# Feed-forward layer of a two-layer decoder on one core: weights in two float32r halves instead of three bfloat16 pieces

## The chip, the core and the metric

The kernel runs on one of the eight cores of a Trainium2 chip. A core has TensorE (PE: matrix multiplications, with weight loads shown apart as PEld), VectorE (DVE), ScalarE (ACT), GpSimd (POOL) and SyncE (SP), which here issues the DMAs. Each engine works through its own list of instructions in order; engines wait for one another on semaphores. The metric is the device time of one execution in microseconds (us). Three runs of the kernel before took 3097.56, 3102.97 and 3102.03 us; the median is 3102.03 us.

## The reference

Eight sequences of 256 tokens with 512 features pass through two decoder layers. Each layer has three sub-layers, and after each of them comes x = layernorm(x + sublayer(x)): windowed self-attention, quantised cross-attention and a GELU feed-forward in the first, a state-space layer with a convolution of four taps, linear attention and a mixture of experts in the second. The change touches the feed-forward:

```python
X = x.reshape(-1, H).astype(jnp.float16)
D = jnp.dot(X.astype(jnp.float32), W0.T) + bias0              # 512 -> 2048
D = jax.nn.gelu(D, approximate=False).astype(jnp.float16)
E = jnp.dot(D.astype(jnp.float32), W1.T) + bias1              # 2048 -> 512
return E.astype(jnp.float16).reshape(B, L, H)
```

The activations are float16 (11 significant bits) and the weights float32 (24 significant bits). float32r, a type that the changed kernel uses, is a float32 whose last 12 bits are zero.

## The kernel before

Eight stages run one after the other: self-attention (names with sa_), projections of the cross-attention (xp_), its heads (xh_), its output (xo_), the feed-forward (gf_), the state space (ss_), linear attention (la_) and the experts (ex_). Each stage is a block of hand-ordered programs, one per engine, and one block begins when every engine has ended the one before. A stage may fetch and prepare for the next one (`ahead`), and leaves its last normalisation to the next one (`behind.late_vector`, `late_pool`, `late_sync`). Batches are the eight sequences.

Feed-forward weights. `W0` and `W1` come in eight chunks of 128x2048 float32 (`fetch_chunk`), and each is split into three bfloat16 pieces whose sum is the float32: `top` (ACT, copies the chunk to bfloat16), `remainder` (DVE, subtracts it), `middle` (ACT, rounds the rest), `lowest` (DVE, subtracts again). Chunks 0 to 5 are split during the cross-attention's output stage, one per batch; chunks 6 and 7 are finished at the start of the feed-forward block. In the output stage each batch passes through one serial loop: SP loads `x` of the next batch into the buffer that the batch before it left, POOL adds the bias to it (L1328), POOL takes the inverse root (L77) for the batch at hand, DVE scales (L1274), SP stores and loads again.

Feed-forward block, for each batch n:

- PE first layer (L1566): 16 feature tiles x 4 contraction tiles x 3 pieces = 192 matmuls, a 128x128 weight tile each with 256 tokens of `xT` moving.
- PE turns the input of batch n+1 (`turn_input`, 8 transposes, L114). It needs `x_loaded`.
- PE second layer (L1579): 16 contraction tiles x 2 token tiles x 3 pieces = 96 matmuls, 128 tokens of `hid` as the loaded operand and 512 columns of `w1` moving.
- ACT copies the turned input to float16 (L1591) and applies GELU to the first layer's result, two tiles at a time (L1598); it writes float16, and PE reads that directly. `hid` has two buffers.
- DVE adds the bias and the residual when the second layer is done (L1622, L1625) and normalises; POOL takes the inverse root (L77). Then SP stores the batch (L1533) and, behind that in its list, loads `x` of batch n+2 (L1529).

Near the end of the block SP also fetches what the state-space stage needs: `w_in` (2 MB), the convolution's weight `w_conv` (4 MB), `w_x`, `w_dt` and `w_out`.

## Time and profile before

| | |
|---|---|
| runs, median | 3102.03 us |
| profiled execution: span from first to last instruction | 3090.6 us |
| mean granted TensorE clock | 0.969 |
| busy: PE / PEld / DVE / ACT / POOL | 91% / 59% / 67% / 48% / 35% |
| feed-forward, first matmul of the first layer | 1389.41 us |
| feed-forward, DVE takes the last result | 1731.72 us |

The profile gives no time of its own for the profiled execution beside its span; the median of the runs is 11.4 us above the span, which is the time around the first and the last instruction. The feed-forward lasts from 1386 to 1732 us, a ninth of the span. "Busy" PE in the profile means that at least one matmul is in flight, so its pace is read from start times, not from busy shares.

### The profile page before, as it was taken

How to read it: one execution, taken by the hardware profiler on the slowest of the kernel's cores; microseconds unless marked ns; L12 is line 12 of the kernel's file. 1: busy time of each engine (PE TensorE's matmuls, PEld its weight loads, DVE VectorE, ACT ScalarE, POOL GpSimd, SP SyncE). 2: the span in 40 equal slices, each digit the busy share in tenths (PEclk: the TensorE clock that was granted, in tenths of full speed). 3: DMA queues.
4: the chain of work that ended last, by engine and by line, in shares of the span. 5: the costliest groups of instructions: out<-in, count | busy, mean ns of one | idle time of the engine just before them, and what ended most of it. 6: DMA issues, size and time to landing. Idle time of an engine off the chain costs nothing. (4 is left out here: it accounts for less than half of the span.)

```text
span 3090.6 us, 49867 instructions
## 1 busy us (share of the span) xinstructions
PE 2803.7 (91%) x18400; PEld 1823.5 (59%) x18400; DVE 2060.7 (67%) x2513; ACT 1492.3 (48%) x2891; POOL 1075.4 (35%) x951
## 2 busy tenths in 40 slices
PE   7999889888888888879999999999997799988997
PEld 5666646444444444437766677777775555555775
DVE  4788766799999999671111069999999533335555
...
GB/s 92 21 41 28 104 88 83 72 171 168 171 167 166 162 169 187 152 177 28 27 27 132 14 67 57 48 50 52 39 45 86 143 67 41 69 16 54 77 86 49
DMA packets 519638, 269.75 MB, mean 87 GB/s; under 512 B 429200, under 2 KB 467216, under 8 KB 517904
## 3 DMA queue, kind: packets, MB, share of 16 engines
...
q8 instruction: 122, 2.00, 0.3%
...
## 5 line engine op out<-in xcount | busy, mean ns | idle before, releaser
L1167 DVE TENSOR_REDUCE xh_top<-xh_seen 128x1 f32<-128x512 f32 (+1 forms) x768 | 631.6, 864 | 45.8 <-PE xh_seen L1069 32.2
L1139 ACT ACTIVATE xh_prob<-xh_sc,xh_bias,xh_scale 128x1024 int16<-128x1024 f32 (+1 forms) x512 | 610.1, 1202 | 68.8 <-PE xh_sc L1069 68.6
L2277 POOL TENSOR_TENSOR ss_state<-ss_du,ss_b_all 128x1024 f32<-128x1024 f32 x128 | 444.3, 3483 | 171.3 <-PE ss_turned L1877 96.1
L1069 PE MATMUL xh_seen<-xh_kT,xh_qT 96*128 96x512 bf16 x1024 | 354.9, 388 | 79.9 <-DVE xh_top L1167 77.6
L2325 DVE TENSOR_TENSOR_SCAN ss_state<-ss_decay,ss_state 128x1024 f32<-128x1024 f32 x128 | 384.4, 3004 | 27.5 <-ACT ss_decay L2127 27.5
L1069 PE MATMUL xh_sc<-xh_kT,xh_qT 96*128 96x512 bf16 x1024 | 310.0, 385 | 1.4 <-ACT xh_prob L1139 1.3
L1193 POOL CAST xh_probT<-xh_pairs 128x2048 int16<-128x2048 uint8 x128 | 242.1, 1891 | 11.2 <-DMA xh_pairs<-xh_prob 1.9
L1069 PEld LDWEIGHTS xh_seen<-xh_kT,xh_qT 96*128 96x128 bf16 x1024 | 89.5, 97 | 241.2 <-DVE xh_top L1167 219.0
L1884 PE MATMUL ss_bank<-ss_xc,hold_w_conv 128*128 128x256 f32 x1024 | 229.3, 379 | 0.7 <-ACT ss_xc L2139 0.7
L2127 ACT ACTIVATE ss_decay<-ss_delta,ss_a 128x255 f32<-128x255 f32 x512 | 211.0, 498 | 0.4
L1884 PEld LDWEIGHTS ss_bank<-ss_xc,hold_w_conv 128*128 128x128 f32 x1024 | 189.9, 189 | 26.4 <-ACT ss_xc L2139 1.1
L1622 DVE TENSOR_TENSOR gf_e<-gf_y_psum,gf_b 128x1024 f16<-128x1024 f32 x8 | 9.8, 1225 | 287.7 <-PE gf_y_psum L1579 287.7
L1093 PEld LDWEIGHTS xh_o<-xh_v_head,xh_probT 128*128 128x128 f16 x4096 | 134.1, 96 | 83.7 <-POOL xh_probT L1193 37.5
L2336 DVE SCALAR_TENSOR_TENSOR ss_acc<-ss_turned,ss_c_t,ss_acc 128x512 f32<-128x512 f32 x256 | 176.4, 729 | 1.1 <-PE ss_turned L1877 1.1
L1566 PE MATMUL gf_hid_psum<-gf_xT,gf_w 128*128 128x256 f16 x1536 | 171.5, 275 | 1.2 <-ACT gf_xT L1591 1.2
L1877 PE MATMUL ss_turned<-ss_ident,ss_state 128*128 128x128 f32 x1024 | 139.3, 279 | 34.1 <-DVE ss_acc L2336 32.3
L1579 PE MATMUL gf_y_psum<-gf_w,gf_hid 128*128 128x512 bf16 x768 | 167.1, 379 | 0.0
L1207 POOL TENSOR_SCALAR xh_low<-xh_top 128x1 f32<-128x1 f32 x256 | 93.1, 364 | 210.3 <-DVE xh_top L1167 209.9
L1566 PEld LDWEIGHTS gf_hid_psum<-gf_xT,gf_w 128*128 128x128 bf16 x1536 | 151.5, 99 | 21.7 <-issue 1.6
L1598 ACT ACTIVATE gf_hid<-gf_hid_psum,gf_b 128x256 f16<-128x256 f32 x128 | 53.7, 471 | 214.1 <-PE gf_hid_psum L1566 214.1
L1877 PEld LDWEIGHTS ss_turned<-ss_ident,ss_state 128*128 128x128 f32 x1024 | 119.6, 144 | 59.4 <-DVE ss_state L2325 28.5
L1093 PE MATMUL xh_o<-xh_v_head,xh_probT 128*128 128x32 bf16 x4096 | 142.5, 177 | 13.3 <-DVE xo_heads_out L1156 8.1
...
## 6 DMA issues: line engine op xcount, KB each, us to landing
...
```

The lines of the kernel that those rows point to most:

```text
L1069: ins = pe.matmul(out[:, c * D:(c + 1) * D], qT[s][:, t * P:(t + 1) * P], kT[s][:, at + c * D:at + (c + 1) * D], start=True, stop=True)
L1093: ins = pe.matmul(o[:, t, :], probT[t % RING][:, b, :].bitcast(F16), v_head[s][:, b, :], start=(b == 0), stop=(b == TT - 1))
L1139: act.activation(out, scores, ACT.Exp, bias=bias[t % RING][:, :], scale=scale[s][:, t:t + 1], accum_out=total[s][:, half, t:t + 1]).then_i ...
L1167: ins = v.tensor_reduce(top[t % RING][:, k:k + 1], scores[:, 0:n], AX.X, ALU.max)\
L1193: g.tensor_copy(probT[t % RING][:, :, :].rearrange("p (b two) q -> p b two q", two=2), pairs[t % RING][:, :, :].bitcast(U8).rearrange("p b ...
L1566: ins = pe.matmul(hid_psum[m // 2 % 3][:, m % 2, :], w0[i][:, c, m * P:(m + 1) * P], xT[:, c, :], start=(c == 0 and i == 0), stop=(c == KD ...
L1877: ins = pe.transpose(turned[r][:, m * P:(m + 1) * P], state[k % RING][:, m, t * P:(t + 1) * P], ident[:, :])
L1884: ins = pe.matmul(out, w_conv[:, k, c, m * P:(m + 1) * P], xc[:, c, k:k + S], start=(k == 0 and c == 0), stop=(k == TAPS - 1 and c == KD - 1))
L2127: ins = act.activation(decay[k % RING][:, m, 1:], delta[s][:, m, 1:], ACT.Exp, scale=a[:, m, k:k + 1])
L2277: g.tensor_tensor(state[k % RING][:, :, :], du[s][:, :, :], spread(b_all[s][:, k, :], KD), ALU.mult)\
L2325: v.tensor_tensor_scan(flat(state[k % RING][:, :, :]), flat(decay[k % RING][:, :, :]), flat(state[k % RING][:, :, :]), 0.0, ALU.mult, ALU. ...
L2336: v.scalar_tensor_tensor(acc[s][:, t, :], turned[(k * TB + t) % BANKS][:, :], c_t[s][:, t, k:k + 1], acc[s][:, t, :], ALU.mult, ALU.add).t ...
```

## The change

Each weight chunk is cut into two halves of 12 significant bits: DVE masks away the low 12 bits (`upper`, an integer AND with -4096), ACT copies this into a float32r tile (`top`), and DVE subtracts the mask's result from the chunk into the second float32r tile (`lower`). `remainder`, `middle` and `lowest` are gone. PE multiplies each activation tile by two halves instead of three pieces. Both operands are float32r now, so the float16 activations are widened by POOL: `widen_input` for `xT` and `widen` for each pair of `hid` tiles. ACT writes the float16 values into `xT_half16` and into a ring of four pairs `hid_half16`. `hid` is now one buffer, which `widen` may overwrite when the second layer of the batch before is done (`y_ps`). POOL's inverse root of batch n-1 stands behind the third `widen` of batch n. Since the weights take more room, `w_conv` lies over `w0`, and its DMA is issued when the first layer of the last batch is done; `w_out` is fetched in the state-space block.

In the output stage's loop (`cross_output`), ACT now does `top` of the chunk before, and DVE does `upper` and `lower` ahead of scaling:

```diff
@@ -1373,8 +1375,7 @@
                 if n + 1 < B:
                     bring(n + 1)
                 if 1 <= n <= ahead.inside:
-                    ahead.middle(act, n - 1)
-                ahead.top(act, n)
+                    ahead.top(act, n - 1)
 
         @block.vector
         def _(v):
...
-                    ahead.remainder(v, n)
+                    ahead.upper(v, n)
+                    ahead.lower(v, n)
                 if n < B - 1:
                     scaled(v, n, chain)
-                if 1 <= n <= ahead.inside:
-                    ahead.lowest(v, n - 1)
-
-
-def gelu_ffn(nc, A, x_in, x_out):
```

The split itself, the semaphores that it uses, and the fetch of a chunk:

```diff
-            _, dram, c = chunks[i]
+            dram, c = chunks[i]
             if i >= 2:
-                sp.wait_ge(rest_ready, ONE + i - 1)
+                sp.wait_ge(low_ready, ONE + i - 1)
...
+        def upper(v, i):
+
+            v.wait_ge(w_loaded[i % 2], ONE + 16 * (i // 2) + 16)
+            if i >= 2:
+                v.wait_ge(top_ready, ONE + i - 1)
+            v.tensor_scalar(uppers[i % 2].bitcast(I32), whole[i % 2][:, :].bitcast(I32), UPPER, None,
+                            ALU.bitwise_and).then_inc(masked, 1)
+
         def top(act, i):
 
-            w, _, c = chunks[i]
-            act.wait_ge(w_loaded[i % 2], ONE + 16 * (i // 2) + 16)
-            act.activation(part(w, c, 0), whole[i % 2][:, :], ACT.Copy).then_inc(top_ready, 1)
-
-        def remainder(v, i):
-
-            w, _, c = chunks[i]
-            v.wait_ge(top_ready, ONE + i + 1)
-            if i >= 2:
-                v.wait_ge(split, ONE + i - 1)
-            v.tensor_tensor(rests[i % 2], whole[i % 2][:, :], part(w, c, 0), ALU.subtract).then_inc(rest_ready, 1)
-
-        def middle(act, i):
-
-            w, _, c = chunks[i]
-            act.wait_ge(rest_ready, ONE + i + 1)
-            act.activation(part(w, c, 1), rests[i % 2], ACT.Copy).then_inc(mid_ready, 1)
-
-        def lowest(v, i):
-
-            w, _, c = chunks[i]
-            v.wait_ge(mid_ready, ONE + i + 1)
-            v.tensor_tensor(part(w, c, 2), rests[i % 2], part(w, c, 1), ALU.subtract).then_inc(split, 1)
+            act.wait_ge(masked, ONE + i + 1)
+            act.activation(part(i, 0), uppers[i % 2], ACT.Copy).then_inc(top_ready, 1)
+
+        def lower(v, i):
+
+            v.wait_ge(masked, ONE + i + 1)
+            v.tensor_tensor(part(i, 1), whole[i % 2][:, :], uppers[i % 2], ALU.subtract).then_inc(low_ready, 1)
```

The feed-forward block (SP, POOL, PE, ACT, DVE):

```diff
-            sp.wait_ge(rest_ready, ONE + len(chunks))
+            sp.wait_ge(low_ready, ONE + len(chunks))
+            sp.wait_ge(top_ready, ONE + len(chunks))
 
             def load(pair, s):
                 sp.wait_ge(x_free[s], ONE + pair)
@@ -1538,11 +1540,39 @@
                 ahead.fetch_inputs(sp)
 
             stream(sp, load, store, fetch_ahead)
+            sp.wait_ge(hid_ps, ONE + B * HALVES)
+            ahead.fetch_conv(sp)
 
         @block.gpsimd
         def _(g):
             behind.late_pool(g)
-            inverse_roots(g, ln, B - 1)
+            g.memset(ln.minus_half[:, :], -0.5).then_inc(ln.half_set, 1)
+            g.wait_ge(ln.half_set, ONE + 1)
+
+            def widen_input(n):
+                g.wait_ge(xT_half, ONE + n + 1)
+                g.wait_ge(hid_ps, ONE + n * HALVES)
+                g.tensor_copy(xT[:, :, :], xT_half16[:, :, :]).then_inc(xT_sb, 1)
+
+            def widen(n, i):
+                g.wait_ge(hid_half, ONE + n * HALVES + i + 1)
+                g.wait_ge(y_ps, ONE + n)
+                g.tensor_copy(hid[:, 2 * i:2 * i + 2, :], hid_half16[:, i % TURNS, :, :]).then_inc(hid_sb, 1)
+
+            widen_input(0)
+            g.wait_ge(low_ready, ONE + len(chunks))
+            g.wait_ge(top_ready, ONE + len(chunks))
+
+            def step(n, root, more):
+                for i in range(HALVES):
+                    widen(n, i)
+                    if i == 2 and root:
+                        inverse_root(g, ln, n - 1)
+                if more:
+                    widen_input(n + 1)
+
+            for n in range(B):
+                step(n, n > 0, n < B - 1)
 
...
 
             def step(n, s, more):
                 pe.wait_ge(xT_sb, ONE + n + 1)
-                pe.wait_ge(split, ONE + KD)
+                pe.wait_ge(top_ready, ONE + KD)
+                pe.wait_ge(low_ready, ONE + KD)
                 for m in range(KF):
                     if m % 2 == 0 and m // 2 >= 3:
-                        pe.wait_ge(hid_sb, ONE + n * HALVES + m // 2 - 2)
+                        pe.wait_ge(hid_half, ONE + n * HALVES + m // 2 - 2)
                     elif m % 2 == 0:
-                        pe.wait_ge(hid_sb, ONE + n * HALVES)
+                        pe.wait_ge(hid_half, ONE + n * HALVES)
                     for c in range(KD):
-                        for i in range(3):
+                        for i in (0, 1):
                             ins = pe.matmul(hid_psum[m // 2 % 3][:, m % 2, :], w0[i][:, c, m * P:(m + 1) * P],
-                                            xT[:, c, :], start=(c == 0 and i == 0), stop=(c == KD - 1 and i == 2))
+                                            xT[:, c, :], start=(c == 0 and i == 0), stop=(c == KD - 1 and i == 1))
                     if m % 2:
                         ins.then_inc(hid_ps, 1)
                 if more:
                     turn_input(n + 1, 1 - s)
-                pe.wait_ge(split, ONE + 2 * KD)
+                pe.wait_ge(top_ready, ONE + 2 * KD)
+                pe.wait_ge(low_ready, ONE + 2 * KD)
                 pe.wait_ge(y_read, ONE + n)
                 for k in range(KF):
                     if k % 2 == 0:
                         pe.wait_ge(hid_sb, ONE + n * HALVES + k // 2 + 1)
+                    half = w1[2 * k // KF]
                     for t in range(TB):
-                        for i in range(3):
-                            ins = pe.matmul(y_psum[:, t, :], hid[s][:, k, t * P:(t + 1) * P], w1[i][:, k, :],
-                                            start=(k == 0 and i == 0), stop=(k == KF - 1 and i == 2))
+                        for i in (0, 1):
+                            ins = pe.matmul(y_psum[:, t, :], hid[:, k, t * P:(t + 1) * P], half[i][:, k % (KF // 2), :],
+                                            start=(k == 0 and i == 0), stop=(k == KF - 1 and i == 1))
                 ins.then_inc(y_ps, 1)
...
         def _(act):
             def turned(n):
                 act.wait_ge(xT_ps, ONE + n + 1)
-                act.wait_ge(hid_ps, ONE + n * HALVES)
-                act.activation(flat(xT[:, :, :]), flat(xT_psum[:, :, :]), ACT.Copy).then_inc(xT_sb, 1)
+                act.wait_ge(xT_sb, ONE + n)
+                act.activation(flat(xT_half16[:, :, :]), flat(xT_psum[:, :, :]), ACT.Copy).then_inc(xT_half, 1)
 
             def step(n, s, more):
-                act.wait_ge(y_ps, ONE + n - s)
                 for m in range(KF):
                     if m % 2 == 0:
                         act.wait_ge(hid_ps, ONE + n * HALVES + m // 2 + 1)
-                    ins = act.activation(hid[s][:, m, :], hid_psum[m // 2 % 3][:, m % 2, :], ACT.Gelu,
-                                         bias=b0[:, m:m + 1])
+                        if m // 2 >= TURNS:
+                            act.wait_ge(hid_sb, ONE + n * HALVES + m // 2 - TURNS + 1)
+                        else:
+                            act.wait_ge(hid_sb, ONE + n * HALVES)
+                    ins = act.activation(hid_half16[:, m // 2 % TURNS, m % 2, :], hid_psum[m // 2 % 3][:, m % 2, :],
+                                         ACT.Gelu, bias=b0[:, m:m + 1])
                     if m % 2:
-                        ins.then_inc(hid_sb, 1)
+                        ins.then_inc(hid_half, 1)
                 if more:
                     turned(n + 1)
 
             turned(0)
             for i in range(p.inside, len(chunks)):
-                middle(act, i)
+                top(act, i)
             steps(act, step)
 
         @block.vector
         def _(v):
             for i in range(p.inside, len(chunks)):
-                remainder(v, i)
+                upper(v, i)
+                lower(v, i)
             behind.late_vector(v)
-            for i in range(p.inside, len(chunks)):
-                lowest(v, i)
 
```

The state space's weights:

```diff
-        w_conv = hold.w_conv = hold.sb("w_conv", [P, TAPS, KD, D])
+        w_conv = hold.w_conv = nc.alloc_sbuf_tensor_at("hold_w_conv", [P, TAPS, KD, D], F32, offset=hold.conv_at)
         w_dt = hold.w_dt = hold.sb("w_dt", [P, D])
         ln = Norm(p)
         w_x = p.sb("w_x", [P, KD, DT + 2 * N])
-        w_out = p.sb("w_out", [P, KD, D])
...
                              allow_slow_non_contiguous=True).then_inc(consts, 16)
             sp.dma_start(a[:, :, :], tiled(A["L1_attn_A_log"])).then_inc(consts, 16)
-            sp.dma_start(w_conv[:, :, :, :].rearrange("p t k n -> p (t k) n"), tiled(A["convT"])).then_inc(conv_loaded, 16)
             sp.dma_start(w_x[:, :, :], tiled(A["L1_attn_W_x"])).then_inc(rest_loaded, 16)
             sp.dma_start(w_dt[:, :], A["L1_attn_W_dt"]).then_inc(rest_loaded, 16)
-            sp.dma_start(w_out[:, :, :], tiled(A["L1_attn_W_out"])).then_inc(rest_loaded, 16)
+
+        def fetch_conv(sp):
+            sp.dma_start(w_conv[:, :, :, :].rearrange("p t k n -> p (t k) n"), tiled(A["convT"])).then_inc(conv_loaded, 16)
 
         def fetch_inputs(sp):
...
+            sp.dma_start(w_out[:, :, :], tiled(A["L1_attn_W_out"])).then_inc(out_loaded, 16)
 
             def step(q, s, post, back, mid, front):
```

The following rows are the engines' own lists. VectorE where the output stage ends and the feed-forward block begins, before (`gf_rest` and `gf_y_out` hold what a split leaves, `gf_w_2` is the third piece; the two branches are the block's border):

```order
L1274 TENSOR_SCALAR xo_y_out<-xo_x,xo_moments,xo_rstd 128x512 x2
L1476 TENSOR_TENSOR gf_w_2<-gf_y_out,gf_w_1 128x2048
L1386 TENSOR_TENSOR xo_x<-xo_y_psum,xo_x 128x1024
L181 UNCONDITIONAL_BRANCH
L1610 UNCONDITIONAL_BRANCH
L1464 TENSOR_TENSOR gf_rest<-gf_whole,gf_w_0 128x2048
L1464 TENSOR_TENSOR gf_y_out<-gf_whole,gf_w_0 128x2048
L1259 BN_STATS xo_stats<-xo_x 128x6 x2
L1263 BN_AGGR xo_moments<-xo_stats 128x2 x2
L1265 TENSOR_SCALAR xo_shifted<-xo_moments 128x2
L1274 TENSOR_SCALAR xo_y_out<-xo_x,xo_moments,xo_rstd 128x512 x2
```

The same place on VectorE now (line numbers are those of the changed kernel; `gf_rest` and `gf_y_out` now hold the upper half):

```order
L1276 TENSOR_SCALAR xo_y_out<-xo_x,xo_moments,xo_rstd 128x512 x2
L1387 TENSOR_TENSOR xo_x<-xo_y_psum,xo_x 128x1024
L183 UNCONDITIONAL_BRANCH
L1646 UNCONDITIONAL_BRANCH
L1464 TENSOR_SCALAR gf_rest<-gf_whole 128x2048
L1475 TENSOR_TENSOR gf_w_second<-gf_whole,gf_rest 128x2048
L1464 TENSOR_SCALAR gf_y_out<-gf_whole 128x2048
L1475 TENSOR_TENSOR gf_w_second<-gf_whole,gf_y_out 128x2048
L1261 BN_STATS xo_stats<-xo_x 128x6 x2
L1265 BN_AGGR xo_moments<-xo_stats 128x2 x2
L1267 TENSOR_SCALAR xo_shifted<-xo_moments 128x2
L1276 TENSOR_SCALAR xo_y_out<-xo_x,xo_moments,xo_rstd 128x512 x2
```

One 128x2048 instruction less stands ahead of the border, and four instead of two stand between the border and the last batch's statistics.

GpSimd in the feed-forward block, before (the loop holds the inverse roots of batches 0 to 6):

```order
L1542 UNCONDITIONAL_BRANCH
L77 TENSOR_TENSOR xo_rstd<-xo_shifted,xo_minus_half 128x2
L143 MEMSET gf_minus_half 128x2
L145 UNCONDITIONAL_BRANCH
L145 ISA
L77 TENSOR_TENSOR gf_rstd<-gf_shifted,gf_minus_half 128x2
```

GpSimd at the same place now:

```order
L1546 UNCONDITIONAL_BRANCH
L79 TENSOR_TENSOR xo_rstd<-xo_shifted,xo_minus_half 128x2
L1549 MEMSET gf_minus_half 128x2
L1555 CAST gf_xT<-gf_xT_half 128x1024
L1560 CAST gf_hid<-gf_hid_half 128x512 x8
L1555 CAST gf_xT<-gf_xT_half 128x1024
L1560 CAST gf_hid<-gf_hid_half 128x512 x3
L79 TENSOR_TENSOR gf_rstd<-gf_shifted,gf_minus_half 128x2
L1560 CAST gf_hid<-gf_hid_half 128x512 x5
```

The first widening of the input stands behind the inverse root that ends the output stage, and the inverse root of a batch stands behind three widenings of the next one.

SyncE at the end of the feed-forward block and the start of the next, before:

```order
L1687 DMA ss_a<-in_L_attn_A_log 128x4x16
L1688 DMA hold_w_conv<-in_convT 128x16x512
L1689 DMA ss_w_x<-in_L_attn_W_x 128x4x160
L1690 DMA hold_w_dt<-in_L_attn_W_dt 128x512
L1691 DMA ss_w_out<-in_L_attn_W_out 128x4x512
L1694 DMA ss_x<-x_after_gelu_ffn 128x2x512
L1533 DMA x_after_gelu_ffn<-gf_y_out 128x2x512
```

SyncE there now:

```order
L1721 DMA ss_a<-in_L_attn_A_log 128x4x16
L1722 DMA ss_w_x<-in_L_attn_W_x 128x4x160
L1723 DMA hold_w_dt<-in_L_attn_W_dt 128x512
L1729 DMA ss_x<-x_after_gelu_ffn 128x2x512
L1535 DMA x_after_gelu_ffn<-gf_y_out 128x2x512
L1726 DMA hold_w_conv<-in_convT 128x16x512
L183 UNCONDITIONAL_BRANCH
L1832 UNCONDITIONAL_BRANCH
L1495 DMA x_after_gelu_ffn<-gf_y_out 128x2x512
L1836 DMA ss_w_out<-in_L_attn_W_out 128x4x512
```

The convolution's weight moved behind the store of batch 6, and `w_out` behind the border.

## Rows read from the trace of the kernel before

**Rows 1.** Stretch; busy us (count) PE, PEld, DVE, ACT, POOL; granted clock, DMA, GB/s.
```profile
1500.00:1600.00 100.00, 100.00 (x663) 64.91 (x662) 10.31 (x18) 16.98 (x36) 1.38 (x2) 1.00 0.07 21
```

**Rows 2.** Waits, 1380 to 1800 us: total, times, longest.
```profile
DVE gf_e L1622 <- PE gf_y_psum L1579: 287.7, 8, 36.1
```

**Rows 3.** Timeline of PE: start, us, instruction, count; feed-forward.
```profile
1389.41 10.80 PE L1566 MATMUL gf_hid_psum<-gf_xT,gf_w 128*128 128x256 f16 x74 [1.19 <-ACT gf_xT L1591]
...
1413.80 20.88 PE L1579 MATMUL gf_y_psum<-gf_w,gf_hid 128*128 128x512 bf16 x96
1434.52 21.12 PE L1566 MATMUL gf_hid_psum<-gf_xT,gf_w 128*128 128x256 f16 x192
1455.48 1.04 PE L114 MATMUL gf_xT_psum<-gf_ident,gf_x 128*128 128x128 f32 x8
```

**Rows 4.** Timeline of PE, float32 matmuls of the state space's start.
```profile
1749.04 27.91 PE L1884 MATMUL ss_bank<-ss_xc,hold_w_conv 128*128 128x256 f32 x128 [0.69 <-ACT ss_xc L2139]
1776.78 0.60 PE L1895 MATMUL ss_bank<-ss_ident,ss_x 128*128 128x128 f32 x4
...
1782.75 1.96 PE L1959 MATMUL ss_bank<-ss_w_x,ss_u 128*128 128x16 f32 x16
1784.55 1.97 PE L1977 MATMUL ss_bank<-ss_dt,hold_w_dt 128*128 128x256 f32 x8
```

**Rows 5.** Timeline of PE, output stage: float32, 512 columns.
```profile
1309.18 7.03 PE L131 MATMUL xo_y_psum<-xo_w,xo_oT 128*128 128x512 f32 x16
1316.05 1.04 PE L1347 MATMUL xo_oT_psum<-xa_ident,xo_heads_out 128*128 128x128 f32 x8
```

**Rows 6.** A weight load and a DVE scaling, by shape: busy us, mean ns.
```profile
L1884 PEld LDWEIGHTS ss_bank<-ss_xc,hold_w_conv 128*128 128x128 f32 x1024 | 189.9, 189 | 26.4 <-ACT ss_xc L2139 1.1 <-issue 0.5
L891 DVE TENSOR_SCALAR xp_k_int<-xp_raw 128x1024 bf16<-128x1024 f32 x8 | 5.6, 694 | 1.2 <-DVE xp_raw L632 0.6
```

**Rows 7.** Timeline of DVE: border of the two stages, end of the feed-forward.
```profile
1382.21 2.29 DVE L1476 TENSOR_TENSOR gf_w<-gf_y_out,gf_w 128x2048 bf16<-128x2048 f32 x1
1384.41 1.22 DVE L1386 TENSOR_TENSOR xo_x<-xo_y_psum,xo_x 128x1024 f32<-128x1024 f32 x1
1386.21 2.29 DVE L1464 TENSOR_TENSOR gf_rest<-gf_whole,gf_w 128x2048 f32<-128x2048 f32 x1 [0.58 <-PEq L181]
...
1390.63 1.28 DVE L1259 BATCH_NORM_STATS2 xo_stats<-xo_x 128x6 f32<-128x512 f32 x2
...
1393.31 1.00 DVE L1274 TENSOR_SCALAR xo_y_out<-xo_x,xo_moments,xo_rstd 128x512 f32<-128x512 f32 x2 [0.81 <-POOL xo_rstd L77]
...
1731.72 1.22 DVE L1622 TENSOR_TENSOR gf_e<-gf_y_psum,gf_b 128x1024 f16<-128x1024 f32 x1 [35.24 <-PE gf_y_psum L1579]
```

**Rows 8.** POOL by line and shape: busy us, mean ns.
```profile
L1184 POOL COPY xh_v_head<-xh_v_int 128x512 bf16<-128x512 bf16 x16 | 9.8, 611 | 0.0
L959 POOL TENSOR_SCALAR xp_k_split<-xp_k_rest 128x1024 bf16<-128x1024 f32 x8 | 22.6, 2823 | 1.6 <-POOL xp_k_rest L957 1.6
L2288 POOL TENSOR_TENSOR ss_acc<-ss_acc,ss_gate 128x1024 f32<-128x1024 f32 x8 | 32.8, 4101 | 13.4 <-DVE ss_acc L2336 13.4
```

**Rows 9.** Timeline of POOL and DVE, batch 2 of the output stage.
```profile
1330.87 2.34 POOL L1328 TENSOR_TENSOR xo_x<-xo_x,xo_b 128x1024 f32<-128x1024 f32 x1 [5.89 <-DMA xo_x<-x_after_self_attention]
1331.22 2.02 DVE L1265 TENSOR_SCALAR xo_shifted<-xo_moments 128x2 f32<-128x2 f32 x1
```

**Rows 10.** Timeline of ACT and SP in the feed-forward.
```profile
1437.34 0.84 ACT L1598 ACTIVATE gf_hid<-gf_hid_psum,gf_b 128x256 f16<-128x256 f32 x2 [22.23 <-PE gf_hid_psum L1566]
1441.42 0.39 SPq L1533 DMA_DIRECT2D x_after_gelu_ffn<-gf_y_out  x1
1442.06 0.40 SPq L1529 DMA_DIRECT2D gf_x<-x_after_cross_attention  x1
```

**Rows 11.** Loads of the feed-forward's input, eight of them.
```profile
DMA to landing us min/median/max: 3.5/4.1/6.8
```

**Rows 12.** DMA issue: count, KB, us to landing.
```profile
hold_w_conv<-in_convT SPq DMA_DIRECT2D x1, 4096.0 KB, 17.7
```

54 lines of the change are left out of this document (34 added, 20 removed).

## The prediction

> **What bounds the kernel now.** I read the stretches of the span first, then the waits, then the timeline of each engine around the feed-forward. In the feed-forward PE has work in flight all the time at the full granted clock, 1.00 of 2.4 GHz, while DVE is busy 10 us in 100 and POOL 1.4 [rows 1]. DVE waits for PE's second layer eight times, 287.7 us in all [rows 2]. PE's pace per matmul and the number of matmuls therefore set the stage. A batch is three pieces in a row [rows 3]: first layer 1434.52 to 1455.48, 20.96 us for 192 matmuls, 109.2 ns each; transposes 1.04 us in flight, of which 0.16 lies over the next piece as with the first layer (21.12 against 20.96), so 0.88; second layer 1413.80 to 1434.52, 20.72 us for 96, 215.8 ns each. Sum 42.56 us, eight times.
>
> **PE, the main term.** Each batch loses 64 of 192 and 32 of 96 matmuls. What stays changes its type, and the trace has no float32r matmul. The nearest rows are float32: an instruction with 256 columns leaves two records, each with a 128x128 float32 load and, by its time, twice 256 columns: 1749.04 to 1776.78 for 128 records, 216.7 ns each [rows 4]. That is the pace of 512 bfloat16 columns, so a float32 load hides behind 512 streamed columns. With only 16 columns the same load paces 1782.75 to 1784.55 for 16 records, 112.5 ns each [rows 4]. The load's floor is thus about 112 ns. I take a float32r matmul as one pass at one column per cycle with a float32 load: first layer 128 x 112.5 = 14.4 us, second 64 x 216.7 = 13.9 us, transposes 0.9, together 29.2 us against 42.56. Eight batches give 8 x 13.4 = -107 us. Lower bound of the first layer's pace is the stream, 109.2 (3 us less in all); upper bound of this case is the record's whole 1.96 us / 16 = 122 ns (10 us more).
>
> The Trainium skill (TensorE: Matmul & The Clock Gate, Weight-path perf modes) says that fast weight load is off for float32 operands, which speaks against this change; its section LDWEIGHTS gives one cycle of 1.2 GHz per column, 107 ns for 128. By that figure the load would just fit under 109.2 ns of stream and the sum would be 3 us lower than mine; the trace's 112.5 ns lies close to it.
>
> **The entry, a new wait.** Before, PE began 1.19 us after it was otherwise ready, on ACT's copy, at 1389.41 [rows 3]. Now the first matmul also needs POOL's `widen_input(0)`. That stands behind POOL's inverse root of the last cross-attention batch, which needs DVE's last statistics, which stand behind four split instructions. A subtraction of 128x2048 goes by at 2.21 us (two in 1386.21 to 1390.63) [rows 7]. The mask has one input and an immediate: 1.2 us if it goes as L891 does (694 ns for 1024, so 533 more for the next 1024), 2.3 us if as the subtraction [rows 6, 7]; I take 1.2, as the form is nearer. From the start of the statistics to the scaling took 1390.63 to 1393.31, 2.7 us [rows 7]. The border moves too: `lowest` ahead of DVE's last addition goes (1382.21 to 1384.41, -2.2 us) [rows 7]. But in the output stage's serial loop `upper` now stands ahead of scaling, and DVE and POOL keep each other out: a 128x2 operation of DVE took 2.02 us while POOL added the bias [rows 9]. Stepping through the seven rounds with 1.2 us more ahead of each scaling, I get scaling 0.5 to 2 us later and 0.6 at the end, so the border comes 1.5 us earlier (bounds 2.2 earlier, 1 later): DVE goes on at 1384.7. Then 2 x (1.2 + 2.2) = 6.8 to 1391.5, 2.7 to 1394.2, DVE's scaling holds POOL off for 1.0 [rows 7], and widening 128x1024 takes 1.2 (twice the COPY of 512 in 611 ns; 4.1 at the slowest row for 1024) [rows 8]. First matmul at about 1396.5: +7 us, bounds +5 and +13. ACT's two `top` copies run beside it. The slow start of the first layer (1389.41 to 1413.80 - 0.88, 23.5 us against 21.0) [rows 3] I leave as it is.
>
> **The widenings in the loop.** Eight of 128x512 and one of 128x1024 per batch: 8 x 0.61 + 1.2 = 6.1 us of POOL's 29 (at the slowest row 8 x 2.05 + 4.1 = 20.5) [rows 8]. PE's first layer makes a pair every 1.8 us, GELU of a pair is 0.84 [rows 10], and the ring holds four pairs; the second layer asks for the first pair at 15.3 us and then for one each 1.7 us. So hidden. The single `hid` costs nothing: its first overwriting waits for the second layer that ends just as the next first layer begins.
>
> What comes late next is `x`. Its load stands on SP behind the store, so behind POOL's root. Counted from the first layer's start, the store went out at 6.90 and the load at 7.54 (1441.42 and 1442.06 less 1434.52) [rows 3, 10], with 21 us to spare to land in 4.1 [rows 11]. Now: third pair at 3 x 1.8 + 0.2 = 5.6, GELU 6.4, its widening 7.1, root 7.8, scaling 8.9, load 9.6, landed 13.7; PE wants it at 14.4. With DVE's scaling and the fourth widening shutting each other out it is 15.6, 1.2 late. Six loads are concerned, batches 2 to 7. I take 0.3 each and 2.4 for batch 7, whose load shares the queue with `w_in` and may take 6.8 [rows 11]: +4 us, bounds 0 and +12.
>
> **Costed at nothing.** Splitting: ACT does 8 copies in place of 16, DVE 8 masks in place of 8 subtractions; hidden by the loop of SP, POOL and DVE apart from what is counted. `w_conv`: issued when the last first layer ends; the last second layer (13.9) and the way to the first convolution (DVE's take at 1731.72 to 1749.04, 17.3 [rows 4, 7]) give 31 us of cover against 17.7 to land with five other transfers [rows 12]. Without that cover PE would stand one us per us. SP is past its wait before the block ends, and the store of the last batch comes behind a transfer that has landed by then. `w_out` (1 MB) is asked for by a wait after the first batches only.
>
> **Sum.** -107 + 7 + 4 = -96 us on the profiled span of 3090.6, so 2995. The median of the runs lies 11.4 above the span before (3102.0), and I keep that distance: **3006 us**. Its own bounds: 3102 - 110 + 5 + 0 = 2997 and 3102 - 97 + 13 + 12 = 3030.
>
> **Rivals.** (1) Float32r streams at half a column per cycle, since each column is four bytes for either operand. For it: the float32 records show 216.7 ns for 256 columns [rows 4] and (1316.05 - 1309.18) / 16 = 429 ns for 512 [rows 5], never less. Against it: an instruction leaves two such records, so four passes in all, and a single pass of exact 12-bit halves is what is left of them. It would give 128 x 0.2167 + 64 x 0.429 + 0.9 = 56.1 us a batch, +13.5 x 8 = +108, with the entry +7: 3217 us, slower. It decides from 159 ns per 256 columns on (256 x 0.159 + 0.9 = 41.6 a batch, entry paid). The Trainium skill (Perfetto Trace Analysis, Engine Utilization) halves TensorE's output rate for the low and high passes of float32; if float32r counted as such, this rival would be its result. The float32 rows agree with that note and say nothing of float32r.
>
> (2) The load does not hide. One float32 load is recorded with 189 ns [rows 6]; if each matmul of the first layer took that, it would be 24.3 + 13.9 + 0.9 = 39.1 a batch, -28 + 7: 3081 us. Against it stands the 112.5 ns of rows 4, where loads overlap each other.
>
> (3) POOL's cast to float32r goes like its slowest row, 4.0 ns per column [rows 8]. It is still no bound (21 of 29 us), but the root comes at 9.8, scaling behind the fourth widening at 12.9, `x` lands at 17.9, 3.5 late six times, and the entry is 3 later: -107 + 10 + 21, 3026 us.
>
> **Chances.** Forecast 0.70, (3) 0.12, (1) 0.10, (2) 0.06, no visible effect or another mishap 0.02. The range 2992 to 3040 holds the first two and leaves out (1), (2) and the rest. Within 0.2% (6 us) a measurement of this kernel can't tell a difference. Faster 0.88, same 0.02, slower 0.10.
>
> **What would show it.** In the changed profile: records of 128x256 float32r about 112 ns apart and of 128x512 about 217; a batch in 29.2 us plus its wait; one record per instruction. The first matmul near 1396.5, with POOL's cast as the releaser and DVE's four split instructions before it. Transposes of batches 2 to 7 waiting for the DMA of `gf_x` by 0 to 1.5 us. POOL casts of 128x512 at 0.6 us. The first convolution released by ACT as before and not by `hold_w_conv`. The prediction is wrong if the 256-column pace is above 122 ns, or if POOL or `x` holds PE for more than 2 us a batch.

## The result, and the profile after

The changed kernel takes 3009.66 us, the median of four runs (3002.76 to 3020.28), beside 3099.8 us for the kernel before in the same session (3096.49 to 3102.97). The ratio is 0.9714, 95% interval 0.9694 to 0.9733. The forecast was 3006 us in a range of 2992 to 3040.

The profiled execution has a span of 3018.5 us and is the run of 3020.28 us. The first lines are the answer to [rows 1]: one stretch in the middle of the feed-forward; the columns are the stretch, its length, busy us with counts for PE, PEld, DVE, ACT and POOL, the granted clock, the DMA share and GB/s.

```profile
1500.00:1600.00 100.00, 100.00 (x648) 91.59 (x647) 15.65 (x27) 27.06 (x57) 22.81 (x33) 1.00 0.17 54
```

PE is still in flight all the time at full clock. Its weight loads have gone from 64.91 to 91.59 us in 100, and POOL from 1.38 to 22.81. The wait that marked the stage is shorter (total, times, longest), 185.1 us where [rows 2] had 287.7:

```profile
DVE gf_e L1657 <- PE gf_y_psum L1612: 185.1, 8, 32.9
```

The timeline of PE answers [rows 3]: start, duration, instruction, count.

```profile
1380.38 1.94 PE L116 MATMUL gf_xT_psum<-gf_ident,gf_x 128*128 128x128 f32 x8 [12.99 <-PEq L183]
1391.17 18.07 PE L1597 MATMUL gf_hid_psum<-gf_xT,gf_w 128*128 128x256 f32 x128 [8.85 <-POOL gf_xT L1555]
1409.07 1.04 PE L116 MATMUL gf_xT_psum<-gf_ident,gf_x 128*128 128x128 f32 x8
1409.86 7.54 PE L1612 MATMUL gf_y_psum<-gf_w_first,gf_hid 128*128 128x512 f32 x32
1417.24 7.42 PE L1612 MATMUL gf_y_psum<-gf_w_second,gf_hid 128*128 128x512 f32 x32
1424.50 15.51 PE L1597 MATMUL gf_hid_psum<-gf_xT,gf_w 128*128 128x256 f32 x128
1440.18 1.09 PE L116 MATMUL gf_xT_psum<-gf_ident,gf_x 128*128 128x128 f32 x8 [0.17 <-DMA gf_x<-x_after_cross_attention]
...
1455.65 15.52 PE L1597 MATMUL gf_hid_psum<-gf_xT,gf_w 128*128 128x256 f32 x128
1471.01 1.03 PE L116 MATMUL gf_xT_psum<-gf_ident,gf_x 128*128 128x128 f32 x8
1471.80 7.53 PE L1612 MATMUL gf_y_psum<-gf_w_first,gf_hid 128*128 128x512 f32 x32
1479.16 7.42 PE L1612 MATMUL gf_y_psum<-gf_w_second,gf_hid 128*128 128x512 f32 x32
1486.42 3.76 PE L1597 MATMUL gf_hid_psum<-gf_xT,gf_w 128*128 128x256 f32 x30
```

There is one record per float32r instruction (printed f32): 128 in the first layer, 64 in the second. From start to start, a batch without a wait is 1486.42 - 1455.65 = 30.77 us: first layer 15.36 (128 x 120.0 ns), transposes 0.79, second layer 14.62 (64 x 228.4 ns). Before it was 42.56.

The border of the two stages is where the feed-forward block begins, marked here by PE's first transposes: 1386.28 before, 1380.38 now. What stands around it on DVE, ACT and POOL answers [rows 7]; all lines are of the changed kernel:

```profile
1380.32 1.23 DVE L1464 TENSOR_SCALAR gf_rest<-gf_whole 128x2048 int32<-128x2048 int32 x1 [0.58 <-PEq L183]
1381.58 2.29 DVE L1475 TENSOR_TENSOR gf_w_second<-gf_whole,gf_rest 128x2048 fp32r<-128x2048 f32 x1
...
1388.96 0.17 DVE L1267 TENSOR_SCALAR xo_shifted<-xo_moments 128x2 f32<-128x2 f32 x1
1389.93 1.84 DVE L1276 TENSOR_SCALAR xo_y_out<-xo_x,xo_moments,xo_rstd 128x512 f32<-128x512 f32 x2 [0.80 <-POOL xo_rstd L79]
...
1382.36 1.02 ACT L1624 ACTIVATE gf_xT_half<-gf_xT_psum 128x1024 f16<-128x1024 f32 x1 [17.16 <-PE gf_xT_psum L116]
...
1389.20 0.69 POOL L79 TENSOR_TENSOR xo_rstd<-xo_shifted,xo_minus_half 128x2 f32<-128x2 f32 x1 [11.64 <-DVE xo_shifted L1267]
1389.84 0.10 POOL L1549 MEMSET gf_minus_half<- 128x2 f32 x1
1390.00 1.04 POOL L1555 CAST gf_xT<-gf_xT_half 128x1024 fp32r<-128x1024 f16 x1
```

ACT's input for the cast was there at 1383.4. POOL stood 11.64 us behind DVE's statistics, and those stood behind four split instructions. In the loop, POOL and SP (the answer to [rows 10]) look like this; the first layer starts at 1424.50:

```profile
1431.35 0.61 POOL L1560 CAST gf_hid<-gf_hid_half 128x512 fp32r<-128x512 f16 x1 [1.30 <-ACT gf_hid_half L1634]
1431.93 0.69 POOL L79 TENSOR_TENSOR gf_rstd<-gf_shifted,gf_minus_half 128x2 f32<-128x2 f32 x1
1433.27 0.85 POOL L1560 CAST gf_hid<-gf_hid_half 128x512 fp32r<-128x512 f16 x1 [0.66 <-ACT gf_hid_half L1634]
...
1433.83 0.39 SPq L1535 DMA_DIRECT2D x_after_gelu_ffn<-gf_y_out  x1
1434.47 0.40 SPq L1531 DMA_DIRECT2D gf_x<-x_after_cross_attention  x1
```

Last, the convolution (KB and us from issue to landing, then PE), which answers [rows 12] and [rows 4]:

```profile
hold_w_conv<-in_convT SPq DMA_DIRECT2D x1, 4096.0 KB, 13.5
...
1657.93 4.37 PE L1921 MATMUL ss_bank<-ss_xc,hold_w_conv 128*128 128x256 f32 x19 [0.69 <-ACT ss_xc L2178]
```

Issued at 1625.02, the weight is there at 1638.5, 19 us ahead of its first use, and ACT releases that use as before.

### The profile page after: what moved, and what is told of

Its sections match the earlier page's. It is cut to its first block and busy times, and to the rows that moved or that the text cites. A ratio compares the mean times of both kernels' runs of the same rounds, so it can differ in the third digit from the quotient of the medians.

```text
span 3018.5 us, 48494 instructions
## 1 busy us (share of the span) xinstructions
PE 2717.1 (90%) x17608; PEld 1825.5 (60%) x17632; DVE 2049.7 (68%) x2513; ACT 1476.6 (49%) x2883; POOL 1109.3 (37%) x1023
## 5 line engine op out<-in xcount | busy, mean ns | idle before, releaser
L2316 POOL TENSOR_TENSOR ss_state<-ss_du,ss_b_all 128x1024 f32<-128x1024 f32 x128 | 432.2, 3388 | 187.1 <-PE ss_turned L1914 111.2
L1071 PEld LDWEIGHTS xh_sc<-xh_kT,xh_qT 96*128 96x128 bf16 x1024 | 96.1, 98 | 77.5 <-ACT xh_prob L1141 4.6
L1657 DVE TENSOR_TENSOR gf_e<-gf_y_psum,gf_b 128x1024 f16<-128x1024 f32 x8 | 9.8, 1224 | 185.1 <-PE gf_y_psum L1612 185.1
L1597 PE MATMUL gf_hid_psum<-gf_xT,gf_w 128*128 128x256 f32 x1024 | 126.7, 287 | 8.8 <-POOL gf_xT L1555 8.8
L124 PE MATMUL ex_up<-ex_xeT,ex_w 128*128 128x256 bf16 x1024 | 123.9, 275 | 9.5 <-DVE ex_xeT L2965 9.5
```

Source lines behind the costliest of these rows:

```text
L1071: ins = pe.matmul(out[:, c * D:(c + 1) * D], qT[s][:, t * P:(t + 1) * P], kT[s][:, at + c * D:at + (c + 1) * D], start=True, stop=True)
L1597: ins = pe.matmul(hid_psum[m // 2 % 3][:, m % 2, :], w0[i][:, c, m * P:(m + 1) * P], xT[:, c, :], start=(c == 0 and i == 0), stop=(c == KD ...
L2316: g.tensor_tensor(state[k % RING][:, :, :], du[s][:, :, :], spread(b_all[s][:, k, :], KD), ALU.mult)\
```

## The experiments

Each ran beside the kernel before on its chip. All but two start from the changed kernel. "Last take" is DVE's take of the feed-forward's last result (`gf_e`).

**Does the saving survive the stages behind?** In the first pair of profiles the last take moved by 92.1 us (1731.72 to 1639.6), the end of the span by only 72.1. Both kernels were profiled a second time, the changed one first.

> The changed kernel once more, unaltered. Its profile has the feed-forward ending 92 us earlier than before, but the span only 72 us shorter; 19 us are given back between the first convolution and the end, in stages that the change does not touch, and its four runs spread over 17 us. Theory A: this is a state of the later stages that varies from execution to execution (where TensorE's granted clock falls), so a second profile has the same feed-forward (first matmul about 11 us after the border, batch 30.8 us, 92 us gained by the first convolution, each to 1 us) and another loss behind it, 0 to 20 us. Theory B: the moved weight or the other memory layout slows the state space and what follows, so the loss of 19 us comes again, stage by stage (3.4 in the state space, 4.4 by the last of linear attention, 11 in the experts).

3015.42 us, ratio 0.9702 (0.9678 to 0.9727); last take 1636.9, span 3012.6.

> The kernel before, run again for a second profile. In its first profile the time from DVE's take of the feed-forward's last result to the end of the span was 1358.9 us; in the profiles with the changed feed-forward it was 1368 to 1379, although the stages behind the feed-forward are the same but for two transfers. Theory A: the stages behind the feed-forward vary between executions (their granted clock does), and the first profile of the kernel before was at the quick end. It expects a span of 3095 to 3108 us here, with 1366 to 1382 from that take to the end, and the take itself at 1731 within 3. Theory B: the change slows the later stages by 10 to 17 us (another place of w_conv, w_out fetched later, or the clock after a less loaded stage). It expects 1356 to 1362 again. Ratio of times 1.000 within 0.002 by both.

3109.78 us, ratio 1.0007 (0.9996 to 1.0019); last take 1730.5, span 3100.3. From the last take to the end it is now 1369.8 us, where the first profile had 1358.9: the same code, 10.9 us apart. For the changed kernel that stretch is 1378.9, 1375.7 and, below, 1375.2; with the variants below that start from it and keep the place of `w_conv`'s transfer it is 1368.2 to 1378.3, and with the old pieces and `w_conv` late 1373.4. Theory A holds in this: one execution differs from the next by 11 us there, so two profiles can't tell a loss. All three profiles of the changed kernel do lie above both of the kernel before. But both profiles of the kernel before caught quick executions: the second took 3102.06 us, 7.7 below the median of its ten runs, and with 7.7 us more its stretch would be 1377.5, no shorter than those of the changed kernel (an estimate; it takes the 7.7 us to lie in that stretch). The medians are the better witness: they differ by 90.1, 95.3 and 89.6 us in three sessions (below for the third), and the feed-forward with its entry, from DVE's first addition of the output stage to the last take, by 91.2 (423.2 and 423.0 against 332.2, 331.7 and 331.8). A steady loss of more than some 5 us would show; one of a few us stays open.

**The main term.** Half of the float32r matmuls left out: the lower halves of the weights take no part in either layer. The edit is the same in both layers (`stop` moves with it):

```diff
-                        for i in (0, 1):
+                        for i in (0,):
```

> TensorE multiplies by the upper halves only (the lower halves are made but left out of both layers). Theory A (matmul pace bounds a batch, and behind it lies the load of x): first layer 64 x 119.3 ns = 7.6 us, second 32 x 228.8 = 7.3, transposes 0.9, 15.8 us in sum; but x lands only 11.7 us after the first layer's start (third pair's GELU 3.9, widening 4.5, root 5.2, scaling 6.8, load 7.6, landing 4.1 later), so transposes wait 4 us and a batch takes 19.9 us: 87 us less in all than the changed kernel. Rival 1: no wait for x, 15.8 us, 120 us less. Rival 2: POOL or ACT bounds the batch already at 30.8 us: nothing gained.

2938.8 us, ratio 0.9453 (0.9423 to 0.9484). The timeline of its PE:

```profile
1409.48 7.83 PE L1597 MATMUL gf_hid_psum<-gf_xT,gf_w 128*128 128x256 f32 x64
1422.44 1.97 PE L116 MATMUL gf_xT_psum<-gf_ident,gf_x 128*128 128x128 f32 x8 [5.13 <-DMA gf_x<-x_after_cross_attention]
1424.06 5.01 PE L1612 MATMUL gf_y_psum<-gf_w_first,gf_hid 128*128 128x512 f32 x16
1428.90 3.79 PE L1612 MATMUL gf_y_psum<-gf_w_second,gf_hid 128*128 128x512 f32 x16
1432.53 3.03 PE L1597 MATMUL gf_hid_psum<-gf_xT,gf_w 128*128 128x256 f32 x24
```

The pace per matmul stays 120 ns, so the number counts. The whole is 76.6 us shorter than the changed kernel beside it (3015.42), where 87 were expected; the rivals had 120 and nothing. `x` is the wait that was reckoned: with a first layer of 7.7 us its load is up to 5.1 us late in a batch, 27.1 us in six. The rest lies behind the wait. The granted clock is 0.50 from 1422 to 1424 and 0.76 from 1424 to 1429, so the transposes take 1.62 us in place of 0.79, and the first 16 matmuls of the second layer 4.84 before the next 16 take 3.63. The six batches with a wait last 22.7 us in the mean: 15.8 of work at full pace, 4.5 of waiting, 2.4 of slower work.

**Load or stream?** The first layer's pace is above the load's floor of my reckoning, 112.5 ns. The same work was done in twice as many matmuls of 128 columns (token tile outermost, the same weights loaded twice):

```diff
-                    for c in range(KD):
-                        for i in (0, 1):
-                            ins = pe.matmul(hid_psum[m // 2 % 3][:, m % 2, :], ..., xT[:, c, :], ...)
+                    for t in range(TB):
+                        for c in range(KD):
+                            for i in (0, 1):
+                                ins = pe.matmul(hid_psum[m // 2 % 3][:, m % 2, t * P:(t + 1) * P], ...,
+                                                xT[:, c, t * P:(t + 1) * P], ...)
```

> The first layer's matmuls are each cut into two with 128 moving columns, so 256 a batch, each with its own 128x128 float32r load; everything else as changed. The measured pace is 119.3 ns for 256 columns and 228.8 for 512, 10 and 13 ns over the 16-bit pace. Theory A (a fixed addition of about 11 ns per matmul): 55 + 11 = 66 ns each, first layer 16.9 us, 1.6 us more a batch, 13 us in all. Theory B (the load of a 4-byte tile is a floor of 112 ns, as 16-column float32 matmuls show): 256 x 112.5 = 28.8 us, 13.5 us more a batch, 108 us in all.

3143.11 us, ratio 1.0111 (1.0074 to 1.0148). Its timeline, and two stretches with the granted clock behind the busy times:

```profile
1465.05 28.70 PE L1598 MATMUL gf_hid_psum<-gf_xT,gf_w 128*128 128x128 f32 x256
1493.58 1.06 PE L116 MATMUL gf_xT_psum<-gf_ident,gf_x 128*128 128x128 f32 x8
```

```profile
1392.60:1447.20 54.60, 54.60 (x256) 54.60 (x257) 0.57 (x2) 7.16 (x15) 4.30 (x7) 0.50 0.06 20
1465.00:1493.60 28.60, 28.60 (x258) 28.56 (x257) 5.58 (x9) 5.88 (x14) 4.94 (x8) 1.00 0.12 38
```

28.53 / 256 = 111.4 ns at 128 columns: halving the stream gained 8.6 ns, and then the load decides. In batch 0, with the clock at 0.50 all through, the same 256 matmuls took 54.67 us, 213.6 ns each: the load's floor goes with the clock. That is why the whole is 127.7 us above the changed kernel beside it and not 108: seven batches are 13.2 us longer, the first 36.8 in its first layer alone. The next run asks what lies between 128 and 512 columns: the first layer in 192 and 64 columns, the second in 384 for all contraction tiles and then in 128.

```diff
+                    for lo, hi in ((0, 192), (192, S)):
...
+                for lo, hi in ((0, 384), (384, D)):
```

> The changed kernel with every tile of the first layer computed in 192 and then 64 columns (8 matmuls each), and the second layer in 384 columns for all 16 contraction tiles, then in 128. Nothing is left out. So far a float32r matmul took 111.4 ns at 128 columns, 119.8 at 256 and 228.8 at 512. Theory A (above the load's floor a matmul costs the stream and a fixed addition, 10 ns + 0.427 ns per column by the two points): 192 columns would be 92 ns, so the load's 111.4; 384 columns 174 ns; 64 and 128 columns 111.4. Theory B (load and stream disturb each other, so that the sum near the crossing rounds up and the fixed addition exists only when a load runs beside): 192 columns clearly over 111.4, 115 or more, and 384 columns 170 or less (0.4167 x 384 + 3 = 163).

One run, 3177.36 us. PE's timeline, second layer of its second batch and first layer of its third, at clock 1.00:

```profile
1497.42 5.79 PE L1614 MATMUL gf_y_psum<-gf_w_first,gf_hid 128*128 128x384 f32 x32
1503.06 5.71 PE L1614 MATMUL gf_y_psum<-gf_w_second,gf_hid 128*128 128x384 f32 x32
1508.60 3.68 PE L1614 MATMUL gf_y_psum<-gf_w_first,gf_hid 128*128 128x128 f32 x32
1512.12 3.74 PE L1614 MATMUL gf_y_psum<-gf_w_second,gf_hid 128*128 128x128 f32 x32
1515.70 28.72 PE L1598 MATMUL gf_hid_psum<-gf_xT,gf_w 128*128 128x192 f32 x256
1544.25 1.09 PE L116 MATMUL gf_xT_psum<-gf_ident,gf_x 128*128 128x128 f32 x8
```

384 columns: 11.18 / 64 = 174.7 ns, where A's line gives 174. 128 columns: 110.9. The mix of 192 and 64: 28.55 / 256 = 111.5, and were 192 columns 115 it would be 113. Theory A holds: a float32r matmul here takes the larger of about 111 ns (load) and about 11.6 ns + 0.423 ns per column (the line through 120.0 and 228.4, which gives 174.2 at 384 columns). The 16-bit rows give 2.6 ns + 0.416 [rows 3]. Why float32r lies 11 ns above them at 256 columns and 13 at 512 was not taken further; it stays open.

**POOL's widenings.** Each is done twice in a row, those of the input likewise:

```diff
-                g.tensor_copy(hid[:, 2 * i:2 * i + 2, :], hid_half16[:, i % TURNS, :, :]).then_inc(hid_sb, 1)
+                g.tensor_copy(hid[:, 2 * i:2 * i + 2, :], hid_half16[:, i % TURNS, :, :]).then_inc(again, 1)
+                g.wait_ge(again, ONE + n * HALVES + i + 1)
+                g.tensor_copy(hid[:, 2 * i:2 * i + 2, :], hid_half16[:, i % TURNS, :, :]).then_inc(hid_sb, 1)
```

> The changed kernel with each of POOL's widenings done twice in a row (both write the same tile), which adds 8 x 0.61 + 1.04 = 5.9 us of POOL's work per batch, 47 us in all, and a semaphore step between the two. Theory A (POOL is under cover, the prediction's step): PE's batch stays at 30.8 us; the only term is that the inverse root, and with it the load of x, comes about 2 us later, which makes x late by up to 2 us in batches 2 to 7, and the entry 1.1 us longer: +1 to +14 us, 3016 to 3030. Rival (POOL paces the second layer, or the exclusion of DVE by POOL stretches it): +47 us in the whole, 3062 or more.

3017.64 us, ratio 0.9715 (0.9693 to 0.9737), as the changed kernel in the other sessions (0.9702 to 0.9714). The first wait of its PE for `x`, and a batch behind it:

```profile
1440.50 1.09 PE L116 MATMUL gf_xT_psum<-gf_ident,gf_x 128*128 128x128 f32 x8 [0.80 <-DMA gf_x<-x_after_cross_attention]
...
1455.98 15.52 PE L1601 MATMUL gf_hid_psum<-gf_xT,gf_w 128*128 128x256 f32 x128
```

47 us of work added on POOL show as 1.2 us of waits for `x` in the whole stage. From the first addition to the last take it is 333.7 us against 331.9 in the mean of the changed kernel. POOL is under cover with room to double; the rival (+47) falls.

**The entry.** First the statistics and the scaling of the cross-attention's last batch ahead of the splits:

```diff
+            behind.late_vector(v)
             for i in range(p.inside, len(chunks)):
                 upper(v, i)
                 lower(v, i)
-            behind.late_vector(v)
```

> VectorE finishes the last normalisation of the cross-attention before it splits chunks 6 and 7 instead of behind them. Theory A (the entry waits for four split instructions through POOL's inverse root and widen_input): the first matmul comes 6.9 us earlier against the border, about 4 us behind it instead of 10.8, and the whole is 7 us shorter. Rival: the second layer of batch 0 then waits for chunks 6 and 7, or TensorE starts at the lower clock for longer, and at most 2 us are left of it.

3008.56 us, ratio 0.9688 (0.9659 to 0.9718). Its PE and POOL:

```profile
1378.59 1.94 PE L116 MATMUL gf_xT_psum<-gf_ident,gf_x 128*128 128x128 f32 x8 [12.63 <-PEq L183]
1384.33 8.48 PE L1597 MATMUL gf_hid_psum<-gf_xT,gf_w 128*128 128x256 f32 x48 [3.80 <-POOL gf_xT L1555]
1393.68 9.85 PE L1597 MATMUL gf_hid_psum<-gf_xT,gf_w 128*128 128x256 f32 x80 [0.88 <-ACT gf_hid_half L1634]
...
1382.37 0.69 POOL L79 TENSOR_TENSOR xo_rstd<-xo_shifted,xo_minus_half 128x2 f32<-128x2 f32 x1 [6.59 <-issue]
```

The first matmul comes 5.7 us after the border in place of 10.8, but ACT's copies (`top`), which wait for DVE's masks, now end later and stand ahead of the first GELU, and PE waits for that. From the first addition to the last take it is 328.0 us, 3.9 less than the changed kernel and not 7. The second step took this away too: POOL's widening ahead of the inverse root, ACT's copies behind the GELU of the first and the second pair.

```diff
-            behind.late_pool(g)
...
             widen_input(0)
+            behind.late_pool(g)
...
+                    if m in tops:
+                        top(act, tops[m])
...
+            tops = {2: p.inside, 4: p.inside + 1}
+            step(0, 0, True)
+            tops = {}
```

> The changed kernel with another order at the entry of the feed-forward: DVE's statistics and scaling of the last cross-attention batch stand ahead of the two chunks that are split there, POOL's first widening ahead of that batch's inverse root, and ACT's two copies to float32r behind GELU of the first and the second pair. Nothing is left out. Theory A (what delays PE is the order of POOL and ACT alone): first matmul 2.5 to 4 us after the border in place of 10.7, no wait for ACT's gf_hid_half, so the feed-forward ends 7 to 8 us earlier: 3007 to 3009 us. Rival (the clock and POOL's wait for the splits take it back): PE starts early, but its first layer stays at the low granted clock, and widen of the first pair waits for the splits (some 12 us after the border), which is still in time for the second layer: gain 4 us or less, as with the statistics alone.

3017.33 us, ratio 0.9712 (0.9691 to 0.9733), though its first matmul came 5.1 us after the border and its last take at 1632.6. The changed kernel had not run in that session, so a small gain could not be told; the next two ran side by side:

> The reordered entry once more (DVE's statistics first, POOL's widening ahead of the inverse root, ACT's copies behind the first GELUs), with more rounds, against the changed kernel in the same call. In its first profile DVE took the feed-forward's last result 325.9 us after its first addition of the output stage, against 332.3 and 331.7 in two profiles of the changed kernel. Theory A: that gain of 6 us stays to the end, ratio 0.002 below that of the changed kernel (0.9695 if that has 0.9714). Rival: later stages take it back, equal ratios within 0.001.

> The changed kernel itself, in the same call, as the measure for the two others: ratio 0.970 to 0.972, batch 30.8 us, first matmul 10.7 us after the border. From DVE's take of the last result to the end 1366 to 1380 us, since the kernel before has shown 1359 and 1370 in two profiles: were it 1376 or more in every profile of this kernel, the later stages would be slower by the change.

Reordered 3011.78 us, ratio 0.9692 (0.9670 to 0.9713); the changed kernel 3016.65, ratio 0.9707 (0.9687 to 0.9727). PE and POOL of the reordered kernel:

```profile
1381.43 1.94 PE L116 MATMUL gf_xT_psum<-gf_ident,gf_x 128*128 128x128 f32 x8 [12.86 <-PEq L183]
1386.51 17.53 PE L1597 MATMUL gf_hid_psum<-gf_xT,gf_w 128*128 128x256 f32 x128 [3.14 <-POOL gf_xT L1554]
...
1385.18 0.10 POOL L1548 MEMSET gf_minus_half<- 128x2 f32 x1 [6.57 <-issue]
1385.34 1.04 POOL L1554 CAST gf_xT<-gf_xT_half 128x1024 fp32r<-128x1024 f16 x1
```

The feed-forward ends 5.7 us earlier (326.1 us from the first addition to the last take, against 331.8), where 7 to 8 were expected, and the median is 4.9 lower. The intervals overlap, and in the first of its two sessions no gain was seen, so in the time of the whole it is likely, not shown; in the traces it is there both times (325.9 and 326.1). By the traces it is the quickest of the complete versions; by the times it can't be told from the first step, whose ratio was 0.9688. What is left of the entry is POOL itself: its MEMSET waits for nobody, and starts 3.75 us after the border.

**The convolution's weight.** First that part of the change alone, on the kernel before (its three pieces kept): `w_conv` issued after the last first layer, `w_out` in the state-space block.

```diff
             stream(sp, load, store, fetch_ahead)
+            sp.wait_ge(hid_ps, ONE + B * HALVES)
+            ahead.fetch_conv(sp)
```

> The kernel before with only the last part of the change: the transfer of w_conv is issued when the last first layer is done, behind the store of batch 6, and w_out is fetched in the state-space block. The feed-forward keeps its three bfloat16 pieces. Theory A (the prediction's step, costed at nothing): the ratio is 1.000 within 0.002, the transfer has landed some 20 us before the first convolution, which is still released by ACT's ss_xc. Theory B (the fetch costs something in the stages behind it): the time from DVE's take of the last result to the end of the span grows by 10 to 17 us over that of the kernel before in the same call, ratio 1.003 to 1.005.

3108.46 us, ratio 0.9999 (0.9987 to 1.0011). The transfer landed in 13.6 us, and the first convolution was still released by ACT. Then the cover taken away, in the changed kernel:

```diff
-            sp.wait_ge(hid_ps, ONE + B * HALVES)
-            ahead.fetch_conv(sp)
...
             behind.finish(sp)
+            p.fetch_conv(sp)
             sp.dma_start(w_out[:, :, :], tiled(A["L1_attn_W_out"])).then_inc(out_loaded, 16)
```

> The changed kernel with the transfer of w_conv issued only in the state-space block, behind the landing of the feed-forward's last store, ahead of w_out. In the profile of the changed kernel that place on SP is at 1652.2, the transfer took 13.5 us by itself, and the first convolution starts at 1657.9. Theory A (the prediction's condition: without cover PE stands one us per us): issue near 1652, landing 1666 to 1669 with w_out and x beside it, the first convolution released by the DMA of w_conv 8 to 12 us later than now: +8 to +12 us, ratio 0.003 to 0.004 above that of the changed kernel in the same call. Rival (the state-space stage gives the delay back, since its first batch waits for other engines anyway): the first convolution late by the same, but the stage's end by less than 3 us.

3030.85 us, ratio 0.9755 (0.9731 to 0.9779), +14.2 on the median of the changed kernel in the same session. PE's line:

```profile
1666.20 24.14 PE L1920 MATMUL ss_bank<-ss_xc,hold_w_conv 128*128 128x256 f32 x103 [9.01 <-DMA hold_w_conv<-in_convT]
```

The first convolution is 7.6 us later than in the run beside it (1666.20 against 1658.6), the stage's last scaling 11.4 later, the span 12.8. So the delay is not given back, it grows. The stretch right behind, 1665 to 1685, has a granted clock of 0.89 where the changed kernel has 1.00, in one profile of each; that this is the cause is not shown. Theory A's place and releaser are confirmed. Its sizes are not quite: the convolution is 7.6 us late where it had 8 to 12, and the whole 14.2 where it had at most 12.

## Why the prediction was right

Its sum was -107 + 7 + 4 = -96 us at the end of the feed-forward; the profile has -92.1, and the same three terms as measured give -94.4 + 1.8 + 0.2 = -92.4. The mechanism is the one told, but that the sum came so near is luck in part: the main term saved 12.6 us less than forecast, and entry and `x` cost 9.0 us less.

**The main term was mis-sized.** "128 x 112.5 = 14.4 us" is 15.36, and "64 x 216.7 = 13.9 us" is 14.62: 30.77 a batch in place of 29.2, so 8 x 11.8 = -94.4 in place of -107. I took the floor from float32 loads with 16 columns and the stream from float32 records, and the stream of float32r turned out to cost its own addition (11 ns over the 16-bit pace at 256 columns). The floor itself was right: 111.4 ns measured at 128 columns. 120.0 ns lies within the bounds I gave for the first layer (109.2 to 122), 228.4 ns above the one value I gave for the second; I had no bounds there, and should have had.

The section LDWEIGHTS of the Trainium skill (TensorE: Matmul & The Clock Gate) puts the load at 107 ns for 128 columns; the runs show 111.4 at clock 1.00 and 213.6 at 0.50. For 256 and 512 columns its section Back-to-back issue gap gives 262 and 518 cycles, 109.2 and 215.8 ns, as the gap of an isolated matmul, and about 131 ns at 512 columns for a stream of loads and matmuls. The trace has such a stream and bears out the first pair for float16 and bfloat16 [rows 3], not the 131 ns; float32r lies 11 and 13 ns above that pair.

**The entry.** Predicted: first matmul at 1396.5, +7. Measured: 1391.17, +1.8. The mechanism is the one told (POOL's cast the releaser, DVE's four split instructions ahead of it), the mask cost 1.23 us as taken (1.2), the cast 1.04 (1.2). Two pieces were off, 4.4 us at the border and 1.0 behind it. The border came 5.9 us earlier, not 1.5, and so outside my bound of 2.2: 1.2 of it was there at the output stage's first addition, and the rest is the output stage, 77.8 to 73.1 us, in each of the profiles (77.8, 78.0 and 80.1 with the old split, 73.1, 73.1 and 72.8 with the new). Scaling is later in the first rounds as reckoned. But `low_ready` comes before scaling, and SP's load of the next chunk goes out earlier against it. The round where this shows most has, in the changed kernel (L1456, L1330) and in the one before (L1449, L1328):

```profile
1333.26 0.37 SPq L1456 DMA_DIRECT2D gf_whole<-in_W1T  x1
1344.38 2.34 POOL L1330 TENSOR_TENSOR xo_x<-xo_x,xo_b 128x1024 f32<-128x1024 f32 x1 [8.29 <-DMA xo_x<-x_after_self_attention]
...
1335.46 0.37 SPq L1449 DMA_DIRECT2D gf_whole<-in_W1T  x1
1346.87 2.36 POOL L1328 TENSOR_TENSOR xo_x<-xo_x,xo_b 128x1024 f32<-128x1024 f32 x1 [10.88 <-DMA xo_x<-x_after_self_attention]
```

The chunk is asked for 2.2 us earlier, and the `x` that follows on the same queue, issued at 1338.10 as before (1338.00), lets POOL begin 2.5 us earlier. This round is 2.6 of the 4.7 us. The order of the transfers as its cause is a reading of the profiles; no run takes it away. I had stepped through DVE and POOL and left the transfers' landing as it was. Behind the border I had POOL's cast wait for DVE's scaling, and it was the other way round: DVE's scaling took 1.84 us in place of 1.00 [rows 7], the cast was not delayed.

The Trainium skill (SBUF — State Buffer, SBUF: two separate sides) calls the port that DVE and GpSimd share an exclusive lock that goes to whoever starts first, for the whole instruction. The trace agrees that one waits for the other: the two records that take 1.00 us alone [rows 7] take 1.84 while POOL casts for 1.04. It does not agree on who waits: by the records DVE's scaling started at 1389.93 and POOL's cast at 1390.00, and DVE was the one held up.

**The slow start of the first layer** was left as it is, and stayed: 17.9 us against 15.4, before 23.5 against 21.0, 2.5 both times.

**`x`.** Predicted +4, measured 0.2 in all. Store and load went out 9.33 and 9.97 us after the first layer's start (I had 8.9 and 9.6), landing takes 4.2 in the median, so 14.2; PE asks at 15.4 and not at 14.4, since the main term was slower. In the batch with the wait of 0.17 us the landing took 5.7. The slack of about a microsecond is real: doubled widenings made 1.2 us of waits, and in the run with half the matmuls `x` was the bound.

**Costed at nothing:** the widenings (0.61 us each as taken) are confirmed by the run that doubles them, `w_conv` and `w_out` by the run that moves them alone and by the releaser of the first convolution. The splits have no run of their own; the output stage that holds six of the eight chunks became shorter, not longer.

**The distance to the span.** "The median of the runs lies 11.4 above the span before", and I read this as time around the first and last instruction. It isn't: the changed kernel's span of 3018.5 belongs to a run of 3020.28, 1.8 above. The profiled execution of before was some 10 us quicker than the median of its runs, in the stages behind the feed-forward. The reason given for it was wrong, but to keep the distance is to take the 96 us off the median of the runs, 3102.0, and that was sound.

**The rivals.** (1) and (2), half a column per cycle and a load that doesn't hide, fall with the pace: 120 ns, where they asked for 216.7 and 189. (3), a slow cast, falls with 0.61 us.
